# Softmax denominators in an attention stage: inverted in compact form and spread by DMA, with the context product on GpSimd

## The reference, cut to what matters

```python
NH, NEG = 8, -1e30                       # B=16 batches, D=256 channels, T=512 positions
q  = transpose(x) @ Wq.T                 # queries, keys and values are the same qh
qh = q.reshape(B, T, NH, 32).transpose(0, 2, 1, 3)
scores = scale * einsum('bhqd,bhkd->bhqk', qh, qh)
logits = (scores * cmask + (1.0 - cmask) * NEG) * rmask
attn = softmax(logits, axis=-1)
ctx  = einsum('bhqk,bhkd->bhqd', attn, qh)
out  = ctx.transpose(0, 2, 1, 3).reshape(B, T, D) @ Wo.T
```

## Time and profile before

| | us |
|---|---|
| median of 3 runs | 2060.32 (2059.29 to 2061.53) |
| the profiled execution's own time | 2059.99 |
| its span, first to last instruction | 2058.2 |
| attention stage in it | 0 to about 735 |
| TensorE busy | 1922.2 (93%) |
| VectorE busy | 1082.7 (53%) |
| ScalarE busy | 709.4 (34%) |
| GpSimd busy | 620.0 (30%) |
| mean granted clock of TensorE | 0.964 |

### The profile page before, as it was taken

The page is one execution under the profiler, slowest core; times in us unless marked ns, Lnnn a source line. Parts: engine busy times, 40 slices in busy tenths (PEclk is TensorE's granted clock), DMA queues, the critical chain, the costliest instruction groups (busy, mean ns, idle before and its releaser), DMA issues. The chain is left out here.

```text
span 2058.2 us, 30150 instructions
## 1 busy us (share of the span) xinstructions
PE 1922.2 (93%) x10324; PEld 1416.7 (69%) x10325; DVE 1082.7 (53%) x1723; ACT 709.4 (34%) x1276; POOL 620.0 (30%) x444
## 2 busy tenths in 40 slices
PE   4999999999999869899999999979999999999995
PEld 2444444444444347799999999868888888888874
DVE  3788878887888548443444433343423323242334
ACT  1566666666666623232333332231010101011000
POOL 3556566666665526211111111100101001010101
PEclk6899999999999969999999999989999999999998
DMA  7776767676765063422333232162302112130204
GB/s 125 111 115 100 111 96 130 101 108 98 128 90 73 21 226 97 150 91 100 124 124 111 83 115 82 67 182 73 102 21 82 41 61 66 36 102 0 93 26 143
DMA packets 117831, 195.83 MB, mean 95 GB/s; under 512 B 11264, under 2 KB 43008, under 8 KB 117776
## 3 DMA queue, kind: packets, MB, share of 16 engines
q1 hardware_dynamic: 106736, 158.94, 34.4%
q0 software_dynamic: 11040, 36.18, 6.1%
HBM read 100.68 MB, written 43.25 MB: 70 GB/s over the span
## 5 line engine op out<-in xcount | busy, mean ns | idle before, releaser
L420 DVE TENSOR_REDUCE maxcol<-ps_m 128x1 f32<-128x512 f32 x512 | 336.9, 681 | 138.5 <-PE ps_m L562 133.4
L337 ACT ACTIVATE e<-ps_e 128x512 f32<-128x512 f32 x512 | 297.3, 596 | 186.5 <-PE ps_e L557 185.7
L148 POOL TENSOR_TENSOR e<-e 128x2048 f32<-128x2048 f32 x64 | 225.6, 3524 | 179.0 <-ACT e L337 178.9
L1384 DVE TENSOR_TENSOR s_h_f<-s_silu,s_ps_u 128x512 f32<-128x512 f32 x77 | 52.9, 688 | 393.5 <-PE s_ps_u L1456 344.0
L562 PE MATMUL ps_m<-kside,qside 97*128 97x512 f32 x512 | 224.3, 443 | 34.7 <-DVE maxcol L420 19.1
L1326 POOL DMA_INDIRECT s_chosen<-routed,s_slot_now x64 | 61.6, 962 | 620.9 <-DVE s_total L1430 609.6
L557 PE MATMUL ps_e<-qside,kside 98*128 98x512 f32 x512 | 236.8, 465 | 3.3 <-ACT e L337 2.1
L557 PEld LDWEIGHTS ps_e<-qside,kside 98*128 98x128 f32 x512 | 96.8, 190 | 191.8 <-ACT e L337 158.7
L1352 ACT ACTIVATE s_silu<-s_ps_g 128x512 f32<-128x512 f32 x77 | 46.0, 598 | 528.8 <-PE s_ps_g L1456 521.3
L1053 DVE TENSOR_TENSOR e_h_f<-e_silu,e_ps_h 128x256 f32<-128x256 f32 (+1 forms) x108 | 45.2, 418 | 250.1 <-ACT e_silu L894 250.1
L562 PEld LDWEIGHTS ps_m<-kside,qside 97*128 97x128 f32 x512 | 101.1, 197 | 80.6 <-DVE maxcol L420 54.6
(11 more groups left out here) (233 smaller groups left out, 4189.0 us busy)
## 6 DMA issues: line engine op xcount, KB each, us to landing
routed<-e_y SPq DMA_DIRECT2D x36, 512.0 KB, 2.8
kside<-q_hi SPq DMA_DIRECT2D x64, 256.0 KB
qside<-qm_hi SPq DMA_DIRECT2D x64, 256.0 KB
x_f<-in_x SPq DMA_DIRECT2D x16, 512.0 KB, 3.5
kside<-q_lo SPq DMA_DIRECT2D x32, 256.0 KB
qside<-qm_lo SPq DMA_DIRECT2D x32, 256.0 KB
attn<-xo SPq DMA_DIRECT2D x32, 256.0 KB, 3.4
keep_rows<-attn SPq DMA_DIRECT2D x8, 1024.0 KB, 5.6
```

What stands on the lines that cost most here:

```text
L148: eng.tensor_tensor(into, into, e[k + 1][:, heads, :], ALU.add).then_inc(done, 1)
L337: act.activation(e[kb][:, g, :], ps_e[g % 2][:, :], ACT.Exp, scale=SCALE).then_inc(e_done, 1)
L420: dve.reduce_max(maxcol[par][:, g * KB + kb:g * KB + kb + 1], ps_m[g % 2][:, :], AX.X).then_inc(max_done, 1)
L1384: dve.tensor_tensor(h_f[:], silu[:], ps_u[:], ALU.mult).then_inc(h_done, 1)
```

## The change

1. VectorE no longer inverts 128 x 512 denominators. ScalarE copies them to one buffer `den`; SyncE copies the 4 rows that differ (partitions 0, 32, 64, 96) to `den_few`, 64 partitions of 32 numbers; VectorE inverts these in one instruction at (3,1) of the step; SyncE copies the result to `over_row`, 4 partitions of 512, and from there, each row 32 times, to `over`, 128 x 512.
2. The product `c_f = num * over` is GpSimd's, the first thing it does in the next step. `context_high` moves from after (0,1) to after (0,2).
3. The mask rows of all batches are made once at the start, 16 partitions each, and the DMAs pick partition b. The waits that guarded the old rows go.
4. The steps are unrolled: no hardware loop, all waits against constants.

```diff
+    den, over = sb("den", [P, T], f32), sb("over", [P, T], f32)
+    den_few, over_few = sb("den_few", [FEW, HG * T // FEW], f32), sb("over_few", [FEW, HG * T // FEW], f32)
+    over_row = sb("over_row", [HG, T], f32)
...
 SyncE, step:
-                bp = (n + 3) // 2 % 2
-                alone(sp, q_split, w + 1, w_in, 32)
-                upto(sp, rows_done, 2 * (b + 1))
+                upto(sp, q_split, w + 1)
...
-                                 words(src[bp][0:1, :]).rearrange("p (a t) -> p a t", a=1).to_broadcast([1, HG, T])).then_inc(stack_in[slot], 16)
+                                 words(src[b:b + 1, :]).rearrange("p (a t) -> p a t", a=1).to_broadcast([1, HG, T])).then_inc(stack_in[slot], 16)
... after the copy of the maxima, before the loads of x and the stores:
+            if known(i, n, -1):
+                w = u - 1
+                sp.wait_ge(den_done, w + 1)
+                sp.dma_start(den_few[:], den[0:P:DK, :]).then_inc(few_in, 16)
+                sp.wait_ge(over_done, w + 1)
+                sp.dma_start(over_row[:], over_few[:]).then_inc(over_row_in, 16)
+                upto(sp, c_done, w)
+                sp.wait_ge(over_row_in, 16 * (w + 1))
+                sp.dma_start(over[:], over_row[:].rearrange("h (a t) -> h a t", a=1).to_broadcast([HG, DK, T])).then_inc(over_in, 16)
 GpSimd, step, ahead of all else:
+            if known(i, n, -2):
+                w, par = u - 2, n % 2
+                pool.wait_ge(over_in, 16 * (w + 1))
+                pool.wait_ge(num_done, w + 1)
+                upto(pool, chi_done, w - 1)
+                pool.tensor_tensor(c_f[par][:], num[par][:], over[:], ALU.mult).then_inc(c_done, 1)
 ScalarE:
-            act.activation(den[par][:], ps_den[:, :], ACT.Copy).then_inc(den_done, 1)
+            upto(act, few_in, 16 * w)
+            act.activation(den[:], ps_den[:, :], ACT.Copy).then_inc(den_done, 1)
...
-                    if (kb, g) == (0, 1) and known(i, n, -2):
+                    if (kb, g) == (0, 2) and known(i, n, -2):
                         context_high(i, n)
 VectorE:
-        def normalise(i, n, at):
-...
+        dve.wait_ge(mask_rows_in, 16)
+        dve.tensor_copy(row_mask[:], rows_f[:]).then_inc(rows_done, 1)
+        dve.tensor_scalar(row_neg[:], rows_f[:], -NEG, NEG, ALU.mult, ALU.add).then_inc(rows_done, 1)
...
-                dve.tensor_copy(row_mask[bp][:], mask_b[bp][0:1, :]).then_inc(rows_done, 1)
-                dve.tensor_scalar(row_neg[bp][:], mask_b[bp][0:1, :], -NEG, NEG, ALU.mult, ALU.add).then_inc(rows_done, 1)
...
+                    if g == 1 and kb == 3 and known(i, n, -1):
+                        dve.wait_ge(few_in, 16 * u)
+                        upto(dve, over_row_in, 16 * (u - 1))
+                        dve.reciprocal(over_few[:], den_few[:]).then_inc(over_done, 1)
...
-        if NI > 3:
-            with eng.Fori(1, NI - 2) as i:
-                for n in range(LOOP_UNITS):
-                    step(i, n)
+        for u in range(before, NU + after):
+            step(u // RING, u % RING)
```

More of the change, by code:

```diff
@@ L24, in attention @@
     STACK_DMAS = 8
-    PARTS = 4
+    FEW = P // 2
     def sb(name, shape, dt):
@@ L49, in attention @@
     mask_b = [sb(f"mask_b{n}", [P, T], f32) for n in range(2)]
-    row_mask = [sb(f"row_mask{n}", [1, T], f32r) for n in range(2)]
-    row_neg = [sb(f"row_neg{n}", [1, T], f32r) for n in range(2)]
+    rows_f = sb("rows_f", [NB, T], f32)
+    row_mask, row_neg = sb("row_mask", [NB, T], f32r), sb("row_neg", [NB, T], f32r)
     q_f = [sb(f"q_f{n}", [P, T], f32) for n in range(2)]
@@ L64, in attention @@
     num = [sb(f"num{n}", [P, T], f32) for n in range(2)]
-    den = [sb(f"den{n}", [P, T], f32) for n in range(2)]
-    wq_f, wo_f = num[0][:].rearrange("p (k d) -> p k d", k=KT), den[0][:].rearrange("p (k d) -> p k d", k=KT)
+    den, over = sb("den", [P, T], f32), sb("over", [P, T], f32)
+    den_few, over_few = sb("den_few", [FEW, HG * T // FEW], f32), sb("over_few", [FEW, HG * T // FEW], f32)
+    over_row = sb("over_row", [HG, T], f32)
+    wq_f, wo_f = num[0][:].rearrange("p (k d) -> p k d", k=KT), den[:].rearrange("p (k d) -> p k d", k=KT)
     c_f = [sb(f"c_f{n}", [P, T], f32) for n in range(2)]
@@ L96, in attention @@
     num_done, den_done, chi_done, o_done = sem("num_done"), sem("den_done"), sem("chi_done"), sem("o_done")
-    max_done, c_done, rd_done, rows_done = sem("max_done"), sem("c_done"), sem("rd_done"), sem("rows_done")
+    max_done, c_done, over_done, rows_done = sem("max_done"), sem("c_done"), sem("over_done"), sem("rows_done")
+    mask_rows_in, few_in, over_row_in, over_in = sem("mask_rows_in"), sem("few_in"), sem("over_row_in"), sem("over_in")
     xhi_done, x_split, q_split, c_split = sem("xhi_done"), sem("x_split"), sem("q_split"), sem("c_split")
@@ L107, in upto, with run_units @@
             eng.wait_ge(s, value)
[L109 to L122, removed]
-        for n in range(LOOP_UNITS):
-            step(0, n)
-        if NI > 3:
-            with eng.Fori(1, NI - 2) as i:
-                for n in range(LOOP_UNITS):
-                    step(i, n)
[L129 to L133, removed]
+    def run_units(step, before, after):
+        for u in range(before, NU + after):
+            step(u // RING, u % RING)
     def known(i, n, off=0, lo=0, hi=NU):
-        if isinstance(i, int):
-            return lo <= RING * i + n + off < hi
-        return True
+        return lo <= RING * i + n + off < hi
     def add_pair(eng, u, pair, heads, done):
@@ L157, in load_x @@
             upto(sp, q_split, UPB * (b - 1))
-            upto(sp, rows_done, 2 * (b - 1))
             upto(sp, x_split, b - 1)
@@ L163, in _ @@
         load_x(0, 0)
+        sp.dma_start(rows_f[:], mask).then_inc(mask_rows_in, 16)
         sp.dma_start(wq_f, wqT.rearrange("(k p) c -> p k c", p=P)).then_inc(w_in, 16)
@@ L169, in _ @@
         sp.dma_start(gate_w[:, :, 0:NE], gates.rearrange("(k p) e -> p k e", p=P)).then_inc(gate_in, 16)
+        sp.wait_ge(rows_done, 2)
         sp.wait_ge(setup, 3)
@@ L205, in step @@
                         sp.dma_start(attn[bass.ds(b * D + half * P, P), :], xo[half][:, :]).then_inc(stored[half], 16)
-        run_units(sp, step, -4, 4)
+        run_units(step, -4, 4)
         for half in range(KT):
@@ L254, in _ @@
         pool.tensor_tensor(x_lo[:], x_f[0][:], x_hi[:], ALU.subtract).then_inc(x_split, 1)
-        run_units(pool, step, -4, 2)
+        run_units(step, -4, 2)
     @block.scalar
@@ L371, in _ @@
         act.activation(x_hi[:], x_f[0][:], ACT.Copy).then_inc(xhi_done, 1)
-        run_units(act, step, -4, 5)
+        run_units(step, -4, 5)
     @block.vector
     def _(dve):
-        def normalise(i, n, at):
[L378 to L391, removed]
         dve.memset(one_f[:], 1.0).then_inc(dve_set, 1)
@@ L431, in step @@
                                     ps_o[:, KT * P:KT * (P + NE)].rearrange("p (h e) -> p h e", h=KT)).then_inc(lg_done, 1)
-        run_units(dve, step, -4, 5)
+        run_units(step, -4, 5)
     @block.tensor
@@ L582, in step @@
                         denominators(u, 0)
-        run_units(pe, step, -4, 5)
+        run_units(step, -4, 5)
 def experts(nc, ctx, sems, keep, attn, w_gate, w_up, w_down, sw_gate, sw_up, held, routed):
```

## The result

The changed kernel takes 2403.81 us (median of 4 runs, 2403.26 to 2404.42) against 2060.12 us before (2059.29 to 2061.53): 1.1665 times as long, 95% interval 1.1648 to 1.1682. The forecast was 2433 us, with a range of 2090 to 2560.

The account below looks back on a forecast made before the run. TensorE was taken to bound attention, with the DMA chain adding a wait in every step: 2060 us plus 30 steps x 11.65 = 350, plus 24 for two end steps, less 1 for the loop, gives 2433 us; range 2090 to 2560.

Parts of the forecast that it names:

- Faster: Rival: `over` transfers in 0.8 us, hidden; VectorE's relief of 0.28 us a step remains; 2051 us; chance 0.10.
- no change: Rival: same fast landing, but colliding halves of the pair addition cost the 0.3 us a step; 2060 us; chance 0.05.
- short wait: Rival: `over` is only spread badly, transfer 3.1 or 2.0 us; 2149 or 2112 us; chance 0.30.
- C: End of GpSimd's product `c_f`: R + 15.5 us, 12.9 us into the next step.
- R: End of VectorE's small reciprocal, itself taken as 0.3 us: 2.65 us ahead of the next step's start on average.
- R to `over_row`: DMA of the small reciprocal's result to 4 partitions: 2.1 us, with 0.1 for the semaphore 2.2 us.
- `over`: Spreading DMA of 256 KB from 4 partitions: 10 us of transfer, 11.9 us with the fixed part.
- tail: After C: VectorE's half of the pair addition ends at C + 4.9, denominators start at C + 5.0; 9.65 us lost a step.
- clock: TensorE's clock falls to half behind the wait: bounds 0 and 5 us a step, taken as 2 us.
- The mask rows: Made once at the start: costed at nothing, covered by the weights' load; 0.8 us without that cover.
- The loop: Unrolling the loop: 1.2 us of gain over 20 units, entered in the sum as 1.
- Stage's end: Two more steps at attention's end, where the chain has less to hide behind: 12 us each, 24 us.

Follow-up runs that it names:

- apart_alone: Changed kernel with the four source rows on partitions 0, 4, 8 and 12, and SyncE issuing nothing behind `over` until it has landed: 2159.45 us, 1.0484.
- alone: Changed kernel with one more wait: SyncE issues nothing behind `over` until it has landed; source rows stay on partitions 0 to 3: 2405.59 us, 1.1683.
- four_dmas: Changed kernel with the `over` DMA cut into four, one source row each, so all 16 engines work; rows stay on partitions 0 to 3: 2378.97 us, 1.1538.
- masks_unrolled: Kernel before with mask rows made once and steps written out; division as before on VectorE, no DMA chain: 2043.44 us, 0.9909.
- unrolled: Kernel before with its loop written out and nothing else: 2058.02 us, 0.9983.
- kept_warm: Changed kernel with 32 repeated TensorE matmuls into `ps_m` at (1,0), to work through the stall: 2393.48 us, 1.1615.

## Why the prediction was right, step by step

**The mechanism** is the forecast one: `c_f` waits for `over` in every step, ScalarE stands at `c_hi` and TensorE behind it. "Faster" and "no change" are out by 344 us. The short wait did not come, but its kernel exists: with the source rows apart and the queue quiet, four engines moved 100 GB/s, 25 each where the rival had worked with 21. C is then R + 7.6, between the rival's 8.6 and 7.5; the time is 2159 against its 2149 and 2112, since R itself lies only 1.6 us ahead of the step on average, held up by `den_few`. It was a fair bound for a transfer that the trace of before didn't show.

**R** (the end of the small reciprocal) was taken 2.65 us ahead of the step; it is 3.0 on average (2.5 and 3.5). The small reciprocal took 0.34 us, taken as 0.3. **R to `over_row`**: 2.0 us to the next issue, taken as 2.2. **`over`**: 12.5 us from issue to product on average, taken as 12.0; 0.6 us of it are the traffic behind it. **C** came out at 12.8 us, forecast 12.9, because a transfer 0.5 us longer and the earlier R and shorter first DMA cancel.

The transfer by itself ran at 26 GB/s, so 10 us as forecast, between the two bounds of 31 and 16 GB/s. This hit was in part luck. Both bounds were scaled by the number of partitions read, and apart_alone reads from four partitions too and moves 100 GB/s, above either bound. It is the place of the four rows that counts; 10 us was a choice within a range from 8.4 to 16 whose reasoning does not hold. By the Trainium skill, page "SBUF — State Buffer", section "Door 1: The DMA port swizzle", partitions 0 to 3 share a port of 27.6 GB/s; the 26 to 27 GB/s above agree, and so does what happened when the rows went to four ports. One sign was wrong as well: the DMA share was to be high while `over` runs, and it is 0.23 in alone, where nothing else runs. Only four_dmas has a high share (0.89) at that rate.

**Behind C** the sum of tail and clock was somewhat too large, and the mechanism of the tail was not the forecast one. The forecast let the denominators wait for VectorE's half of the pair addition and start at C + 5.0, and added 2 us for the clock. The addition did end at C + 4.6, and at full clock the denominators start right behind it, at C + 4.7. But in every step of this kernel the clock is at half, TensorE's own list ends last, and they start at C + 6.2. From there to the end of the step it is 12.6 us instead of 12.4. So the tail was 0.3 us too long, and the clock costs 1.5 and 0.2 us where 2 were put. Together: 12.8 + 6.2 - 8.25 + 0.2 = 10.9 us a step, as measured, against 11.65. That is 22 us over 30 steps, the larger part of the 29 us by which the forecast was too high.

**The mask rows** were costed at nothing at the start; there they were worth some 7 us (masks_unrolled), which is the rest of the miss. **The loop** was put at 1.2 us; the interval of unrolled says 1.6 to 5.6, its two medians 2.2. **SyncE's queue** was said to have room, and it had: its copies' issues took 5.0 and 4.3 us (509.70, and 514.75 behind it) while `over` ran, and no engine waits for their landing in the list of the steady part. **`den_few`** was hidden as said; only the kernels with an earlier reciprocal or a held queue ran into it.

**Stage's end**: forecast 24 us for two steps. From the last numerator copy to the next stage it is 13.7 us longer than before. Only the last unit's chain lies behind that copy, so this is in line with 12 each.

## What to carry to other kernels

Before work is taken off an engine by a DMA, follow the longest chain through it and ask whose list stands behind the waiting instruction; here 6 us of VectorE's work a step, of which TensorE had waited for 1.3, were paid for with 11 us of every engine's time. The broadcast from four neighbouring partitions was slow here with four DMA engines and with sixteen; with the source rows four partitions apart it moved about four times as fast, and it reached its reader soonest when nothing large followed it in the queue. Where a kernel is built to remove one cost, as kept_warm was, read from its trace how far the cost is gone: its mean of 0.3 us a step would hide the 1.5 us that the low clock takes. And of a change in several parts, time the parts: the ones that seemed to be only tidying (mask rows once, product on GpSimd) are a kernel at 0.987 of before.

## What the hardware did that was not expected

- Sixteen DMA engines and four got the same 26 to 27 GB/s from partitions 0 to 3; their busy shares (0.89 and 0.23) tell nothing about what they move.
- With its source rows four partitions apart a transfer of 256 KB took 4.5 us from issue to product with a quiet queue, 5.7 to 6.2 us with SBUF copies issued behind it and 8 to 11 us with the x, mask and attention transfers behind it. Those behind slow the one ahead.
- SyncE's two DMA issues of a unit's first copies took 5.0 us instead of 1.24 to 1.27 while `over` ran: the issue itself is held back.
- The granted clock was 0.50 over the 5 us behind every stall, and the denominators started at C + 6.2 instead of C + 4.7. With 32 extra matmuls in the stall it was 1.00 there in only 3 of 27 steps.
- Two VectorE instructions on one partition took 2.56 and 1.48 us beside GpSimd's, each ending 0.28 us behind one of GpSimd's, and 0.41 us where GpSimd was idle.
